# Where the rounded part of a gelu output is made: ScalarE for every chunk, instead of ScalarE and VectorE in turn

## What is computed

```python
def layer(h, p):
    q = _phi((h @ wq + bq_).reshape(b, s, H, DH))
    k = _phi((h @ wk + bk_).reshape(b, s, H, DH))
    v = (h @ wv + bv_).reshape(b, s, H, DH)
    kv = jnp.einsum('bshd,bshm->bhdm', k, v)
    z = 1.0 / (jnp.einsum('bshd,bhd->bsh', q, k.sum(axis=1)) + 1e-06)
    att = jnp.einsum('bshd,bhdm,bsh->bshm', q, kv, z).reshape(b, s, d)
    h = _ln(h + att @ wo + bo_, g1_, be1_)
    y = jax.nn.gelu(h @ w1 + c1_, approximate=False) @ w2 + c2_
    return (_ln(h + y, g2_, be2_), None)
```

## Time and profile before

| what | value |
|---|---|
| median of three runs | 2071.69 us (2069.89 to 2074.51) |
| the profiled execution | 2067.15 us |
| its span in the trace | 2065.4 us |
| the eight layers, by their instructions | about 225 to 745 us of the span |
| busy in the whole span | PE 87%, DVE 74%, ACT 65%, POOL 32% |
| granted TensorE clock, mean | 0.944 of full |

### The profile page before, as it was taken

How to read it: one execution, slowest core, us unless ns; L and a number is a source line. 1 busy time by engine, 2 the same in 40 slices (tenths; PEclk the granted TensorE clock), 3 DMA queues, 4 the chain that set the end, 5 groups by cost and what they waited for, 6 DMA issues and landing times.

```text
span 2065.4 us, 24716 instructions
## 1 busy us (share of the span) xinstructions
PE 1799.8 (87%) x8806; PEld 1111.0 (54%) x8806; DVE 1536.7 (74%) x2489; ACT 1335.5 (65%) x2121; POOL 655.4 (32%) x735
## 2 busy tenths in 40 slices
PE   8999798888988889997798889997577678988998
PEld 5888466665666657885233335783122233332786
DVE  6888687787877758888766654875999866764786
ACT  6999577676776688997356565555544445566554
POOL 1444211011110013444523321322699442233131
PEclk9999999999999989998799998998899879999999
DMA  3221000000000002220000000200000000000110
GB/s 102 76 78 49 19 19 18 1 18 19 19 18 1 11 11 84 75 69 31 0 1 1 1 1 9 85 21 0 11 3 33 0 1 1 1 1 1 57 56 21
DMA packets 23770, 52.89 MB, mean 26 GB/s; under 512 B 2336, under 2 KB 6816, under 8 KB 23648
## 3 DMA queue, kind: packets, MB, share of 16 engines
q1 hardware_dynamic: 23648, 51.30, 7.8%
HBM read 49.66 MB, written 1.64 MB: 25 GB/s over the span
## 4 chain that ended last, share of the span: by engine, by line
PE 60%; DVE 20%; ACT 15%; issue 3%; POOL 1%; DMA 1%; SPq 0%; POOLq 0%; DVEq 0%; ACTq 0%
PE ps L554 9%; PE ps L556 9%; PE ps L555 9%; PE ps L1362 5%; DVE arena L1986 5%; PE ps L1331 4%; PE ps L786 3%; PE ps L783 3%; DVE arena L1703 2%; PE ps L784 2%; ACT arena L1502 2%; PE ps L1320 2%; PE ps L1350 2%; ACT arena L1451 2%; DVE arena L1977 1%
## 5 line engine op out<-in xcount | busy, mean ns | idle before, releaser
L665 DVE TENSOR_TENSOR hid_lo<-arena,hid_hi 128x512 fp32r<-128x512 f32 x384 | 341.6, 902 | 67.5 <-ACT arena L614 65.5
L1703 DVE TENSOR_REDUCE arena<-ps 128x1 f32<-128x512 f32 (+3 forms) x352 | 219.2, 641 | 82.5 <-PE ps L1335 78.9
L1502 ACT ACTIVATE arena<-ps 128x1024 f32<-128x1024 f32 (+3 forms) x256 | 167.6, 703 | 120.9 <-PE ps L1350 120.6
L554 PE MATMUL ps<-x_hi,w_hi 128*128 128x512 f32 x512 | 208.1, 406 | 3.1 <-DVE arena L757 3.1
L556 PE MATMUL ps<-x_hi,w_lo 128*128 128x512 f32 x512 | 203.4, 397 | 0.0
L555 PE MATMUL ps<-x_lo,w_hi 128*128 128x512 f32 x512 | 203.2, 397 | 0.0
L611 ACT ACTIVATE hid_hi<-ps,wslot 128x512 fp32r<-128x512 f32 x256 | 177.3, 693 | 33.8 <-PE ps L556 6.4
L1616 POOL TENSOR_SCALAR_AFFINE_SELECT arena<-arena 128x256 f32<-128x256 f32 x256 | 108.0, 428 | 283.7 <-ACT arena L1502 281.5
L614 ACT ACTIVATE arena<-ps,wslot 128x512 f32<-128x512 f32 x256 | 175.1, 684 | 0.0
L1331 PE MATMUL ps<-arena 128*128 128x512 bf16 (+3 forms) x512 | 138.5, 328 | 41.0 <-DVE arena L1703 12.7
L635 POOL TENSOR_TENSOR x<-x,arena 128x512 f32<-128x512 f32 x64 | 108.4, 1698 | 146.1 <-DVE arena L626 146.1
(11 more groups left out here) (314 smaller groups left out, 4233.7 us busy)
## 6 DMA issues: line engine op xcount, KB each, us to landing
arena<-gates_dram SPq DMA_DIRECT2D x96, 256.0 KB, 3.6
wslot<-pack_a SPq DMA_DIRECT2D x16, 514.5 KB, 3.6
wslot<-pack_b SPq DMA_DIRECT2D x8, 900.5 KB, 4.6
wslot<-pack_c SPq DMA_DIRECT2D x8, 768.0 KB, 4.5
res<-x_in SPq DMA_DIRECT2D x4, 256.0 KB, 5.1
out_dram<-res SPq DMA_DIRECT2D x4, 256.0 KB, 2.8
con<-consts_dram SPq DMA_DIRECT2D x1, 559.0 KB, 4.0
bc_dram<-arena SPq DMA_DIRECT2D x1, 384.0 KB, 3.2
```

The lines of the kernel that those rows point to most:

```text
L554: pe.matmul(ps[:, bank, :], w1, hi, start=start, stop=False)
L665: dve.tensor_tensor(hid_lo[item % 2][:, k, :], hid32[:, k, :], hid_hi[item % 2][:, k, :].bitcast(F32), ALU.subtract).then_inc(S["hid_ok"], 1)
L1502: act.activation(pt[:, u % NPT, :, 0:n], ps[:, 2 * r:2 * r + 2, 0:n], ACT.Exp, scale=SCALE).then_inc(S["exp_ok"], 1)
L1703: dve.tensor_reduce(neg_max[:, i, heads[0]:heads[-1] + 1:step], ps[:, bank, 0:len(heads) * keys].rearrange("p (m k) -> p m k", k=keys), AX ...
```

## The change

For every chunk, ScalarE now evaluates gelu twice from PSUM: first into `hb_b`, then into `hid_g`. Its wait for `ff2_mm` (which guards the buffer `hb_b` against being overwritten while TensorE reads it) now stands before every chunk of blocks 2 and 3, instead of before those with k of 0 and 2. VectorE makes only the difference; its copy and the semaphore `gelu_hi` are gone.

```diff
-                    if k % 2 == 0:
-                        if b >= 2:
-                            act.wait_ge(S["ff2_mm"], m + b - 1)
-                        act.activation(hb_b[b % 2][:, k, :], up, ACT.Gelu, bias=bias)
+                    if b >= 2:
+                        act.wait_ge(S["ff2_mm"], m + b - 1)
+                    act.activation(hb_b[b % 2][:, k, :], up, ACT.Gelu, bias=bias)
                     act.activation(hid_g[:, b % 2, k, :], up, ACT.Gelu, bias=bias).then_inc(S["gelu_ok"], 1)
...
                     dve.wait_ge(S["gelu_ok"], n + 1)
                     if b >= 2:
                         dve.wait_ge(S["ff2_mm"], m + b - 1)
-                    if k % 2:
-                        dve.tensor_copy(hb_b[b % 2][:, k, :], hid_g[:, b % 2, k, :]).then_inc(S["gelu_hi"], 1)
-                        dve.wait_ge(S["gelu_hi"], 8 * l + 2 * b + k // 2 + 1)
                     dve.tensor_tensor(lb_b[b % 2][:, k, :], hid_g[:, b % 2, k, :],
                                       hb_b[b % 2][:, k, :].bitcast(F32), ALU.subtract).then_inc(S["gelu_lo"], 1)
```

More of the change, by code:

```diff
@@ L183, in build @@
             gated_ok added gv_mm silu_ok q_mm q_act qf_ok kv_mm kv_ok k_act kf_ok kvs_mm kvbd_ok kvt_mm kvt_ok g_mm g_ok cb_ok w_prep den_mm
-            den_ok rz_ok z_bc qz_ok o_mm ff1_mm gelu_ok gelu_hi gelu_lo ff2_mm fin_mm bsq_ok bvar_mm blog_ok brs_ok by_ok mid_sq mid_xc mid_var root_ok root_bc
+            den_ok rz_ok z_bc qz_ok o_mm ff1_mm gelu_ok gelu_lo ff2_mm fin_mm bsq_ok bvar_mm blog_ok brs_ok by_ok mid_sq mid_xc mid_var root_ok root_bc
             h_ok h_hi_ok h_lo_ok mid_ok mid_hi_ok mid_lo_ok x_ok conv_all dl_v dl_log dl_rs
```

## The result

The changed kernel takes 2081.87 us (median of six runs, 2078.51 to 2085.80), the kernel before in the same comparison 2073.01 us (2069.89 to 2074.51). The ratio is 1.0039 with a 95% interval of 1.0020 to 1.0057. Measured again later with twelve runs it was 1.0032 (1.0021 to 1.0044). So it is slower: by 7 to 8 us by the ratios, by 8.9 and 8.4 us by the medians; forecast were 8.8.

A forecast was written before the change was run, and what follows sets the result against it. TensorE bounds the middle of each layer's feed-forward part and waits for ScalarE at two places. Beginning 4.1 us plus end 4.7 us, all else zero, is 8.8 us; 2071.69 + 8.8 = 2080.5 us, range 2075.5 to 2087 us.

The forecast's parts named there:

- What bounds the kernel now: TensorE bounds the feed-forward part's middle; it waits for ScalarE at `ff1(1, 0)` and at the closing squares.
- The beginning: New gelu delays the full gelu of (0, 1), for which `ff1(1, 0)` waits: 4.1 us over eight layers.
- The distance of 1.40 us: Sign: `ff1(1, 0)` starts 1.40 us behind the start of what follows `mid_high(3)` on ScalarE, in every layer.
- The end: New gelu of (3, 3) delays table load, squares and last variance products by 0.59 us a layer, 4.7 us in all.
- The middle: Added gelus between the two places lie in ScalarE's idle time: zero; uncovered, up to 6 x 0.57 us a layer.
- the three chunks of lead: A full gelu ends 0.57 us later, but its bank is wanted three chunks on, some 3.5 us later.
- The removed casts: 64 casts off VectorE, 39.9 us of busy time: worth between 0 and 2.3 us, taken as 0.
- The slack named: Low part of (0, 1) is done 1 us ahead of `ff2(0, 1)`, the earliest place; more slack later.
- The wait for `ff2_mm`: Ahead of chunks with odd k it costs nothing: the same value was already waited for at k of 0.
- Rival 1: TensorE's lower clock lasts longer at the part's beginning: 12.8 us in all, 2093 us; partly, 2085 to 2090 us; chance 0.12.
- Rivals 2 and 3: 2: VectorE's casts delayed TensorE, 2074.8 us, chance 0.10; 3: one of the two places covered, 2076.4 to 2078 us, chance 0.10.
- rival 3: Beginning or end is covered by something unseen; 4.7 to 6 us left, 2076.4 to 2078 us; chance 0.10.

The follow-up runs named there:

- e3_middle: Changed kernel with chunks (0, 1) and (3, 3) back at VectorE, so ScalarE makes 48 of the 64 rounded parts; ratio 1.0000.
- e11_unchanged: The kernel before, unchanged, measured as if it were a changed one; ratio 0.9999.
- e2_start: The kernel before with the rounded gelu moved to ScalarE for chunk (0, 1) alone; ratio 1.0011.
- e1_end: The kernel before with the rounded gelu moved to ScalarE for chunk (3, 3) alone; ratio 0.9997.
- e7_three: Changed kernel with a third gelu, result unused, for each of the 11 chunks from (1, 0) to (3, 2); ratio 1.0269.
- e4_casts_twice: The kernel before with each of VectorE's 64 casts made twice; ratio 0.9998.
- e5_first_cast: Changed kernel with chunks (0, 0), (0, 1) and (3, 3) at VectorE; ratio 1.0001.
- e6_end_twice: The kernel before with two gelus, one unused, added ahead of the full one of chunk (3, 3); ratio 1.0040.
- e8_tail_order: Changed kernel with (0, 0), (0, 1), (3, 3) at VectorE, square(2) moved ahead of the table load, square(3) ahead of root_of(l, 2); ratio 1.0011.

## Why the prediction held

- **Size and sign.** Forecast 2080.5 us, +8.8 us or 0.42%; measured 2081.87 us, +0.39%, and +0.32% when repeated. In the eight layers 8.3 us were found. That the whole time came within 1.4 us of the forecast is partly luck: twelve and more executions of one kernel spread over 7 to 18 us, the forecast stood on a median 1.3 us below that of the comparison, and single places left less in whole times than in the layers.
- **What bounds the kernel now.** Right. The two places where TensorE waits for ScalarE carry all of the change, and e3_middle shows that the rest carries nothing.
- **The beginning, 4.1 us.** Measured 4.0. The sum took four layers at 0.57 us, two a little less, and two at 0.36 where the lower clock covers some; 0.50 us on average were found. The distance of 1.40 us came out in every layer. Which layers have TensorE at its lower clock up to this place differs from execution to execution (two before, three in e11_unchanged, one in the changed kernel, eight in e2_start), so the split into single layers was one execution's; the mean over all traces is 0.54 us.
- **The end, 4.7 us.** Measured 4.3 to 4.4 (0.55 us a layer in both runs of e1_end's kernel, 0.54 in the changed kernel behind `ff1(1, 0)`). The spacing of 0.57 to 0.59 us was the right price, not the 0.69 of the duration. The 0.61 us that the prediction worked out as an estimate from the Trainium skill, "ScalarE: Activation LUTs", section "What ACT_TABLE_LOAD costs", would have given 9.4 in all; the traces have 0.57 to 0.59 us.
- **The middle, zero.** Right for this change (e3_middle). The reason given was incomplete: I named the three chunks of lead as the cover, and e7_three shows that the first limit is another, the square that a variance product waits for.
- **The removed casts, zero.** Right: nothing from 48 fewer (e3_middle), nothing from 64 more (e4_casts_twice). The slack named holds for odd k only (e5_first_cast).
- **The wait for `ff2_mm`, zero.** e1_end carries it at (3, 3), where its price is inside the 0.55 us; nothing of its own is seen.
- **Rival 1, the clock.** Didn't happen in the measured kernel. The granted clock of the feed-forward parts is 0.94 in seven layers and 0.88 in one, before 0.88 in two and 0.94 in the others. These are the rows of layers 3 and 4 after, columns as in the earlier trace rows:

```profile
450.20:479.10 28.90, 25.56 (x104) 19.13 (x105) 18.48 (x29) 24.96 (x39) 3.77 (x2) 0.94 0.00 1
516.00:544.50 28.50, 26.62 (x104) 19.81 (x105) 18.52 (x29) 25.00 (x40) 3.78 (x2) 0.88 0.00 1
```

  A related price is real all the same, at other places: the clock fell behind waits of 1.84 us in two of seven closing parts (e6_end_twice) and behind waits of 2.7 to 3.1 us in all seven (e7_three), 1.1 us each time. So the argument that waits far below the busy stretches around them leave the clock up holds for the 1.26 us of this change, and fails for 1.84 us in part of the layers and for 2.7 us in all.
- **Rivals 2 and 3.** In the layers they fell with e3_middle, e4_casts_twice, e1_end and e2_start: no cast pays back, and both places cost. In whole times rival 3's half is not so clearly excluded, see above.
- **Two marks I set were off.** ScalarE's idle time was to fall by some 35 us; it fell by 27, from 48.2 to 21.1. The 64 gelus take 64 x 0.57 = 36.5 us of it, and the layers, which grew by 8.3 us, give about that much back; that would leave 28. VectorE's busy time was to fall by 40 us and fell by 33: the mean of the differences rose from 710 to 735 ns, 3.7 us in all. Of 128 differences 28 now run beside an instruction of GpSimd (mean 0.89 us), before 14 (0.86 us) and 12 casts; the others take 0.69 us. The remaining 3 us are not explained.

## What to carry to other kernels

Ask of work that is moved to an engine with room not how much it is, but which of its instructions stand ahead of something that another engine waits for: 48 of 64 gelus were free here, and 16 cost all 8 us. Price those at the spacing between starts, and look in the engine's row also for instructions of another kind (a square among gelus), since a backlog reaches them first. Where the rest of a program scatters more than the effect, a stretch between two fixed instructions, read in every repetition of the loop, measures what whole times leave open, but it doesn't vouch for the whole.

## What the runs showed of the hardware

- The recorded duration of gelus grows in a row without gaps, at an unchanged spacing: in e7_three from 0.69 us to 0.88 us over some 25 instructions that start 0.57 us apart, and back to 0.69 behind the first idle time. In the changed kernel it goes up to 0.78. A sum of busy time then counts more than the engine spends.
- TensorE's clock was at its lower level right behind a wait of 1.84 us in two layers and not in five others, with the same matmuls ahead of it (e6_end_twice). Behind waits of 1.73 and 1.74 us for a block of the next layer's keys it fell in one layer of seven (e8_tail_order), behind 1.97 to 2.04 us in the middle of the part in six layers of eight, behind 2.7 to 3.1 us in seven closing parts of seven (both e7_three). Behind 1.25 to 1.29 us it never fell, in 14 closing parts of the changed kernel and its repetition. What decides in the cases between is not shown.
- A cast beside GpSimd's work was stretched to 1.33 us. In the kernel before, the 12 casts beside an instruction of GpSimd took 1.49 us on average and the other 52 took 0.42. Differences are stretched too, to 1.99 us at most before and 1.46 in the changed kernel, where twice as many lie beside GpSimd's work.
